# Attention and routing in one pipeline: scatters in later slots, heads through three banks, row maxima turned by VectorE

## The reference

```python
h = h + attn(_layernorm(h))                 # 16 heads of 32, 4 key/value heads, rotary
scores = softmax(q k^T / sqrt(32)); out = scores v; h += out Wo^T
logits = _layernorm(h) @ gate_w.T           # 64 experts
topk_w, topk_i = top_k(softmax(logits), 6)
slot = place of the token in its expert's buffer of 64, in order of tokens
y = experts(...) combined by topk_w + shared expert
```

## Time and profile before

| | |
|---|---|
| median of 3 runs | 1711.42 us (1710.41 to 1715.89) |
| the profiled execution | 1718.32 us, of it a span of 1716.7 us |
| attention phase in the trace | about 160 to 1078 us |
| experts phase | 1078 us to the end |
| one iteration of the full pipeline | about 103 us |

### The profile page before, as it was taken

How to read it: one execution, slowest core, us unless ns; L and a number is a source line. 1 busy time by engine, 2 the same in 40 slices (tenths; PEclk the granted TensorE clock), 3 DMA queues, 4 the chain that set the end, 5 groups by cost and what they waited for, 6 DMA issues and landing times. The chain is left out here.

```text
span 1716.7 us, 23894 instructions
## 1 busy us (share of the span) xinstructions
PE 1377.3 (80%) x9120; PEld 852.8 (50%) x9120; DVE 764.3 (45%) x1633; ACT 405.0 (24%) x676; POOL 423.5 (25%) x455
## 2 busy tenths in 40 slices
PE   3195788888787887878888850399999999999994
PEld 2194352535345353443534340266666666666663
DVE  7982645454655546656454431323233223232221
ACT  2021132324233242332424310211111111111110
POOL 3000110201115042240504367112222222122221
PEclk6597675878778786878868865599999999999997
DMA  3023211313231242304123140798988989898882
GB/s 96 0 65 84 50 39 35 72 35 96 65 77 36 56 109 56 91 19 107 40 56 91 56 179 21 225 312 252 308 274 297 292 261 331 248 321 273 273 247 33
DMA packets 129837, 239.54 MB, mean 140 GB/s; under 512 B 58056, under 2 KB 64088, under 8 KB 129752
## 3 DMA queue, kind: packets, MB, share of 16 engines
q1 hardware_dynamic: 114232, 214.16, 39.9%
q0 software_dynamic: 15520, 24.22, 7.0%
HBM read 175.66 MB, written 38.90 MB: 125 GB/s over the span
## 5 line engine op out<-in xcount | busy, mean ns | idle before, releaser
L965 DVE TENSOR_REDUCE at_maxes<-at_ps 128x1 f32<-128x384 f32 x384 | 196.5, 553 | 131.9 <-PE at_ps L664 124.8
L819 ACT ACTIVATE bulk<-at_ps 128x1152 f32<-128x1152 f32 x128 | 144.6, 1129 | 419.8 <-PE at_ps L634 418.2
L1330 PE MATMUL mo_ps<-mo_x2s,mo_sgu 128*117 128x384 f32 (+1 forms) x1152 | 221.1, 344 | 0.0
L1330 PEld LDWEIGHTS mo_ps<-mo_x2s,mo_sgu 128*117 128x117 f32 (+1 forms) x1152 | 198.8, 181 | 13.3 <-issue 13.1
L1551 POOL DMA_INDIRECT out_rows<-mo_y,mo_scatter_ix x64 | 91.3, 1427 | 406.0 <-DMA out_rows<-mo_y,mo_scatter_ix 185.8
L664 PE MATMUL at_ps<-at_qb 32*128 32x384 bf16 x384 | 113.6, 419 | 69.4 <-DVE at_maxes L965 55.1
L1131 POOL DMA_INDIRECT slot_table<-at_toki,at_si x144 | 141.7, 984 | 58.4 <-issue 47.1
L1094 POOL TENSOR_TENSOR at_oTs<-at_oT,at_oTs 128x384 fp32r<-128x384 f32 x32 | 31.7, 1004 | 402.9 <-ACT at_oTs L836 402.8
L664 PEld LDWEIGHTS at_ps<-at_qb 32*128 32x128 bf16 x384 | 26.8, 95 | 204.6 <-DVE at_maxes L965 152.0
L625 PE MATMUL at_ps<-WxT,at_xT 128*128 128x512 f32 (+1 forms) x576 | 114.6, 352 | 12.7 <-ACT at_v L866 11.0
L650 PE MATMUL at_ps<-bulk,at_v 128*32 128x384 f32 x768 | 113.0, 683 | 3.2 <-DVE at_oT L979 3.2
(11 more groups left out here) (198 smaller groups left out, 1714.5 us busy)
## 6 DMA issues: line engine op xcount, KB each, us to landing
mo_wgu<-in_L_ffn_w_gate SPq DMA_DIRECT2D x32, 704.0 KB, 6.4
mo_wgu<-in_L_ffn_w_up SPq DMA_DIRECT2D x32, 704.0 KB, 7.7
bulk<-in_L_ffn_w_gate SPq DMA_DIRECT2D x32, 704.0 KB, 7.3
bulk<-in_L_ffn_w_up SPq DMA_DIRECT2D x32, 704.0 KB, 8.6
mo_wd<-in_L_ffn_w_down SPq DMA_DIRECT2D x32, 512.0 KB, 7.9
bulk<-in_L_ffn_w_down SPq DMA_DIRECT2D x32, 512.0 KB, 5.3
at_QT<-at_qhi SPq DMA_DIRECT2D x64, 192.0 KB
rows_scores<-at_x SPq DMA_DIRECT2D x8, 864.0 KB, 3.9
```

The costliest lines, as they stand in the source:

```text
L819: A.activation(PT[:, N % RING, :, :], ps[:, 0:NT, 0:SEQ], ACT.Exp, scale=float(HD) ** -0.5)\
L965: V.tensor_reduce(maxes[:, s, h:h + 1], ps[:, 5 + u % 2, 0:SEQ], AX.X, ALU.max, negate=True)\
L1330: m = M.matmul(ps[0:SW[c], 5 + g, 0:SEQ], sgu[:, wa, g, k, SO[c]:SO[c] + SW[c]], x2s[:, xa, k, :], start=(k3 == 0), stop=(k3 == 3 * KC - 1))
```

## The change

Seven edits, all in `attention_phase`.

1. The scatters of sequence e stand in slots 7 to 12 of GpSimd's program in place of 1 to 6.
2. The routing moves a slot forward: `turn_x2` to slots 2 and 3, `logits` to slot 4, its copy and the largest values to slot 5, the one-hot rows and the mask to slot 6, the gate's exponentials to slot 6.
3. The mask is made by three bf16 additions (three ranks plus three, then two more) in place of a reduction and a cast.
4. `turn_heads` goes through banks 5, 6 and 7; group i waits for group i-3. Groups 0, 1 and 2 stand together.
5. On ScalarE `qhi` comes first, and the bf16 copy follows one group behind, made from `qhi`; the raw products wait for all five (`qb_ready`).
6. The maxima are laid out in 32 columns per part of a sequence, and VectorE transposes them itself in blocks of 32 (`max_row`, behind the maxima of slots 11 and 15). `turn_maxes` and ScalarE's copy are gone, and with them the two waits of TensorE on `mrow_ready`. Four DMAs in place of one put the result into `QT`.
7. On VectorE the first two maxima of a slot come at its head, the next two where all stood before, and in slots 11 and 15 `divide` stands behind those four.

```diff
-        TURN_SLOT = {3: (0, 1), 4: (2, 3)}
+        TURN_SLOT = {2: (0, 1), 3: (2, 3)}
-        STACK = 16 * (2 * 6 + 1)
+        STACK = 16 * (2 * 6 + P // HD)
...
             def stack_max(half):
                 heads = slice(half * NH // 2, (half + 1) * NH // 2)
-                sp.dma_start(QT[SPLIT:QR, heads, :].bitcast(F32), mrow[:, half, :].bitcast(F32)).then_inc(stacked[half], 16)
+                for j in range(P // HD):
+                    sp.dma_start(QT[SPLIT:QR, heads, :].rearrange("p h (s j q) -> p h s j q", s=NT, q=HD)[:, :, :, j, :]
+                                 .bitcast(F32), mrow[HD * j:HD * j + NH // 2, half, :, :]).then_inc(stacked[half], 16)
...
                 if u < 2:
-                    pe.wait_ge(qhi_ready, NTILE * (a + 1))
+                    pe.wait_ge(qb_ready, NTILE * (a + 1))
                     pe.wait_ge(qlo_ready, NTILE * (a + 1))
-                if u == HALF_UNITS:
-                    pe.wait_ge(mrow_ready, 2 * a + 1)
...
             def turn_x(a, k):
                 if k == 0:
                     pe.wait_ge(xn_ready, NT * (a + 1))
-                    wait(pe, mrow_ready, 2 * a)
                     wait(pe, max_ready, UNITS * a)
...
-                if i >= 2:
-                    pe.wait_ge(qlo_ready, NTILE * a + i - 1)
+                if i >= 3:
+                    pe.wait_ge(qlo_ready, NTILE * a + i - 2)
                 for s in range(NT):
-                    m = T.transpose(ps[:, 5 + i % 2, s * P:(s + 1) * P], r1[:, s, r, :], ident[:])
+                    m = T.transpose(ps[:, 5 + i % 3, s * P:(s + 1) * P], r1[:, s, r, :], ident[:])
...
+            def bf16_heads(a, i):
+                r = (REP, 0, 1, 2, 3)[i]
+                act.wait_ge(qhi_ready, NTILE * a + i + 1)
+                A.activation(qb[:, r, :], qhi[:, r, :].bitcast(F32), ACT.Copy).then_inc(qb_ready, 1)
...
+            def max_row(a, half):
+
+                dve.wait_ge(max_ready, UNITS * a + HALF_UNITS * (half + 1))
+                if a >= 1:
+                    dve.wait_ge(stacked[half], STACK * a)
+                V.transpose(mrow[:, half].rearrange("p s h -> p (s h)"), maxes[:, half].rearrange("p s h -> p (s h)"))\
+                    .then_inc(mrow_ready, 1)
...
-                    link(V.tensor_reduce(pos[:], hot[:].rearrange("p (s k) e -> p s e k", s=NT), AX.X, ALU.add), route_step)
-                    V.tensor_copy(mask[:], pos[:]).then_inc(mask_ready, 1)
+                    ranks = hot[:].rearrange("p (s k) e -> p s k e", s=NT)
+                    third = TOPK // 2
+                    link(V.tensor_tensor(threes[:], ranks[:, :, 0:third], ranks[:, :, third:TOPK], ALU.add), route_step)
+                    link(V.tensor_tensor(mask[:], threes[:, :, 0], threes[:, :, 1], ALU.add), route_step)
+                    V.tensor_tensor(mask[:], mask[:], threes[:, :, 2], ALU.add).then_inc(mask_ready, 1)
...
+                    for u in units[0:2]:
+                        row_maximum(a, u)
                     if prev and n - 1 in OUT_SLOT:
                         residual(c, OUT_SLOT[n - 1])
-                    if n % REP == REP - 1:
+                    if n % REP == REP - 1 and n < RAW_FROM:
                         divide(NKV * b + n // REP - 1)
...
-                    for u in units[0:3]:
+                    for u in units[2:4]:
                         row_maximum(a, u)
-                    for u in units[3:]:
+                    if n % REP == REP - 1 and n >= RAW_FROM:
+                        divide(NKV * b + n // REP - 1)
+                    for u in units[4:]:
                         row_maximum(a, u)
+                    if nxt and n in (NH * 3 // 4 - 1, NH - 1):
+                        max_row(a, (n - RAW_FROM) // REP)
...
-                    if prev3 and 1 <= n <= 6:
+                    if prev3 and 7 <= n <= 12:
                         pool.wait_ge(slots_ready, e + 1)
-                        for m in range(3 * (n - 1), 3 * n):
+                        for m in range(3 * (n - 7), 3 * (n - 6)):
```

More of the change, by code:

```diff
@@ L665, in raw @@
                          start=True, stop=True).then_inc(raw_scores, 1)
-            def turn_maxes(a, half):
-                pe.wait_ge(max_ready, UNITS * a + HALF_UNITS * (half + 1))
-                for s in range(NT):
-                    m = T.transpose(ps[0:NH // 2, 5, s * P:(s + 1) * P], maxes[:, s, half * NH // 2:(half + 1) * NH // 2],
-                                    ident[:])
-                m.then_inc(max_turned, 1)
             def turn_x(a, k):
@@ L759, in _ @@
                         turn_x2(d, TURN_SLOT[n][0])
-                    if n == 0 and main:
-                        turn_maxes(b, 1)
-                    if n == NH * 3 // 4 and nxt:
-                        values(G, q)
-                        turn_maxes(a, 0)
                     for u in units[0:2]:
@@ L772, in _ @@
                         turn_heads(a, 1)
-                    if not (n == NH * 3 // 4 and nxt):
-                        values(G, q)
+                        turn_heads(a, 2)
+                    values(G, q)
                     for u in units[2:4]:
@@ L783, in _ @@
                         turn_x(a, 3)
-                    if nxt and n == 7:
-                        turn_heads(a, 2)
                     values(G, q + 1)
-                    if prev2 and n == 5:
+                    if prev2 and n == 4:
                         logits(d)
@@ L820, in exponentials @@
                     .then_inc(probs_ready, 1)
-            def max_row(a, half):
-                act.wait_ge(max_turned, 2 * a + half + 1)
-                if a >= 1:
-                    act.wait_ge(stacked[half], STACK * a)
-                A.activation(mrow[:, half, :], ps[0:NH // 2, 5, 0:SEQ], ACT.Copy).then_inc(mrow_ready, 1)
+            def bf16_heads(a, i):
+                r = (REP, 0, 1, 2, 3)[i]
+                act.wait_ge(qhi_ready, NTILE * a + i + 1)
+                A.activation(qb[:, r, :], qhi[:, r, :].bitcast(F32), ACT.Copy).then_inc(qb_ready, 1)
             def x2_copied(d, k):
@@ L845, in _ @@
                         exponentials(b, n)
-                    if main and n == 0:
-                        max_row(b, 1)
-                    if nxt and n == NH * 3 // 4:
-                        max_row(a, 0)
                     if nxt and n == 0:
@@ L853, in _ @@
                             A.activation(xT[:, 0, k, :], ps[:, 5 + k % 2, 0:SEQ], ACT.Copy).then_inc(xhi_ready, 1)
-                    if prev2 and n == 6:
+                    if prev2 and n == 5:
                         act.wait_ge(logits_ready, d + 1)
@@ L876, in _ @@
                                 act.wait_ge(stacked[1], STACK * a)
-                            A.activation(qb[:, (REP, 0, 1, 2, 3)[i], :], ps[:, 5 + i % 2, 0:SEQ], ACT.Copy)
-                            A.activation(qhi[:, (REP, 0, 1, 2, 3)[i], :], ps[:, 5 + i % 2, 0:SEQ], ACT.Copy)\
+                            A.activation(qhi[:, (REP, 0, 1, 2, 3)[i], :], ps[:, 5 + i % 3, 0:SEQ], ACT.Copy)\
                                 .then_inc(qhi_ready, 1)
-                    if prev2 and n == 8:
+                            if i >= 1:
+                                bf16_heads(a, i - 1)
+                        bf16_heads(a, NTILE - 1)
+                    if prev2 and n == 6:
                         act.wait_ge(gmax_ready, d + 1)
@@ L898, in _ @@
             V.memset(base[:], 0.0)
+            V.memset(maxes[:], 0.0)
             V.memset(ones[:], 1.0)
@@ L953, in q_lo @@
                 dve.wait_ge(qhi_ready, NTILE * a + i + 1)
-                V.tensor_tensor(qlo[:, r, :], ps[:, 5 + i % 2, 0:SEQ], qhi[:, r, :].bitcast(F32), ALU.subtract)\
+                V.tensor_tensor(qlo[:, r, :], ps[:, 5 + i % 3, 0:SEQ], qhi[:, r, :].bitcast(F32), ALU.subtract)\
                     .then_inc(qlo_ready, 1)
@@ L959, in row_maximum @@
                 dve.wait_ge(raw_scores, UNITS * a + u + 1)
-                if u == 0:
-                    wait(dve, max_turned, 2 * a - 1)
-                if u == HALF_UNITS:
-                    wait(dve, max_turned, 2 * a)
-                h = REP * g + r
-                V.tensor_reduce(maxes[:, s, h:h + 1], ps[:, 5 + u % 2, 0:SEQ], AX.X, ALU.max, negate=True)\
-                    .then_inc(max_ready, 1)
+                if u % HALF_UNITS == 0:
+                    wait(dve, mrow_ready, 2 * (a - 1) + half + 1)
+                h = REP * (g % 2) + r
+                V.tensor_reduce(maxes[:, half, s, h:h + 1], ps[:, 5 + u % 2, 0:SEQ], AX.X, ALU.max, negate=True)\
+                    .then_inc(max_ready, 1)
+            def max_row(a, half):
[4 more added lines that the diff above has]
+                    .then_inc(mrow_ready, 1)
             def divide(G):
```

13 lines of the change are left out of this document (7 added, 6 removed).

## The result

The changed kernel takes 1629.42 us (median of 4 runs, 1626.21 to 1636.05), the kernel before 1713.66 in the same session: ratio 0.9515, interval 0.9479 to 0.9551. That is faster, by 84 us by the medians. The forecast was 1641 with a range from 1608 to 1688. The profiled execution took 1628.74 us, of it a span of 1626.9, against 1716.7 before.

What follows compares the result with a forecast made beforehand. TensorE was taken to bound the kernel, losing time to pauses, mostly ended by VectorE, and to a low clock. Iterations gain 75 us, the tail loses 5; net 70 from 1718.3 gives 1648, less 6.9 for the median 1641, range 1608 to 1688.

Steps and rivals of the forecast that it cites:

- Scatters and heads, 2.7 us: Iteration 4, after slot 7's scores: head groups start at once, first raw product at 652.6 in place of 655.26.
- the scatters alone cost 2.0: Slot 7's scores to first raw product: iteration 2, without scatters, takes 9.3 us against 11.3, so scatters cost 2.0.
- Mask and clock, 2.2 and 0.9: From slot 8: the 2.2 us pause before the third raw product goes; the clock rises sooner, gaining 0.9 us.
- The additions, 1.2: VectorE's chain ahead of `q_lo`: the mask's three additions take 1.2 us, between bounds of 0.26 and 2.4.
- Slots 11 and 12, 2.4 and 3.2: Iteration 4: slot 11 falls from 7.79 to 5.4 us, slot 12 from 9.37 to 6.2, if the clock stays up.
- rival A: Clock stays at 1.2 GHz through slots 8 to 12; only 38 of 70 us gained, 1673 us; chance 0.22.
- Slots 15 and 0, taken as 0: Turn to next iteration: `turn_x` 1.7 us sooner, against a longer low clock costing 2.0; taken 0, between -3 and +2.
- Contention, -1.0: `over` in slot 9 and three gate products in slot 10 run beside scatters on VectorE: 1.0 us lost per iteration.
- Rival C: Scatters stop VectorE's maxima in slots 7 to 10, 17.5 us in each of iterations 3 to 7: 1728 us; chance 0.05.
- Iterations and tail: Whole attention phase: iterations -1 to 7 gain 75 us together, the tail after them loses 5, net 70.
- Iteration 0's 9.2 for 9: Iteration 0: slots 11 to 15 fall from 29.74 to 22.4 us, 7.3 less, plus 1.7 with the heads: 9.
- Iteration 7: Iteration 7's gain was put at 3 us, without a working.

Runs made afterwards that it cites:

- the run with the routing back: Changed kernel with the routing a slot later again, mask still by additions and scatters still late: 1628.86 us, ratio 0.9529.
- the second run with the scatters back: Changed kernel with the scatters in slots 1 to 6 again, rerun unchanged in the third group: 1615.45 us, ratio 0.9418 (first run 0.9597).
- the two-bank run: Changed kernel with head transposes through banks 5 and 6 and both copies from PSUM: ratio 0.9670, then 0.9617 (1648.02 us) when rerun.
- the division's run: Changed kernel with `divide` ahead of the maxima in slots 11 and 15 again: ratio 0.9659, then 0.9501 (1627.61 us) when rerun.
- the last run: Changed kernel with next sequence's statistics in slot 4, scatters in slots 7 to 12 only before iteration 8, then 1 to 6: 1611.72 us, ratio 0.9418.
- Four kernels of one group: Changed kernel with one part undone each, first group: scatters back 0.9597, maxima turned by TensorE 0.9751, division ahead 0.9659, two banks 0.9670.

## Why the prediction was right, point by point

**What bounds the kernel.** Right. The experts moved as a block; all of the gain came from TensorE's pauses and clock.

**Scatters and heads, 2.7 us.** Measured 3.0, but the step "the scatters alone cost 2.0" saw half of it. Iteration 2 had no scatters and was 2.0 us quicker to its first raw product, and the same 2.0 stand between a cast of 2.18 and one of 0.18, a cast in the chain ahead of `q_lo`. It begins beside a scatter and ends 0.03 to 0.04 us after the delayed `rope_sum` (647.69 and 647.66 in iteration 4; 542.10 and 542.06 in iteration 3). Late scatters free it (0.18 in the run with the routing back), but so does the routing's move with the scatters in their old slots (0.18 in iterations 2 to 6 of the second run with the scatters back). Of the 3.0 us, the two-bank run keeps 0.9 (11.3 to 10.4); the third bank, with its order of copies, gives 2.1. The prediction gave the pause to the scatters; for it either edit suffices.

**Mask and clock, 2.2 and 0.9.** Slots 8 to 10 gained 2.4 of 3.1 in iteration 4. The pause of 2.2 went as said, so the clock's term was near nothing there; in iteration 3 the same slots gained 5.7 (20.9 to 15.2 us).

**The additions, 1.2.** Measured 1.04. The Trainium skill (VectorE: DVE Perf Modes, tier table) gave an estimate of 0.7 by its two elements a cycle; the trace agrees with that rate (576 elements in 0.46 us, 192 in 0.26), and the fixed part is larger than I counted.

**Slots 11 and 12, 2.4 and 3.2.** Measured 3.0 and 1.5 in iteration 4, and 4.66 and 6.05 us long in iteration 3 where 5.4 and 6.2 were forecast. At full clock slot 12's term is right and slot 11's is 0.7 too small; that the clock stays up was right in two iterations of seven. This is rival A in part: in the other five the clock was low in slot 12, which cost 1.3 to 1.9 us in iterations 1, 4, 5 and 6, about a quarter of A's price. And slot 11's term is not a gain of its own, as the division's run showed: it is the other side of slots 12 and 15.

**Slots 15 and 0, taken as 0.** Measured 1.6. The pause of 2.46 ahead of slot 15's raw products fell to 0.65 and 0.73; against it stands the new wait of `turn_x` of 1.93.

**Contention, -1.0.** Under 0.1 us an iteration: `over` has a mean of 279 ns (260 before), a gate product 287 (266). Rival C fell with it. The Trainium skill (SBUF — State Buffer, who interferes with whom), which the prediction cites, says that a reduction never contends on this chip; the maxima agree (552 ns against 553). It also says that a VectorE operation with two SBUF inputs contends with a GpSimd instruction that reads SBUF. By that rule, the one-hot rows of the last run agree, 2.85 us beside an addition of GpSimd and 1.49 without; that their two inputs are the cause was not tried by itself.

**Iterations and tail.** 72.5 us in iterations -1 to 5, where the working gives 62. Iteration 0's 9.2 for 9 is luck: its slots 11 to 15 were to run at full clock and gain 7.3, but stayed at 0.54 and gained 4.1 (29.74 to 25.62); some 2 more came between its first raw product and slot 11, for which the working has nothing. Iteration 7 gave 8.7 where 3 was taken. Its wait for the mask of 2.2 us is gone, and the granted clock is 1.00 in all of it (0.84 before): that term was mis-sized because it was set down as 3 without a reading of iteration 7's own rows. The tail's -5 was exact at -5.4. The profiled spans lie 89.8 us apart where 70 were summed; of the missing 20, 6.1 are in iteration 3 (slots 8 to 10 as above, and slot 12, 10.84 before and 6.05 after), 5.7 in iteration 7 and 2.9 in iteration 6. The medians came only 12 apart from the forecast, since the profiled execution of before lay 7 above its median and that of after 0.7 below; so much of the closeness is luck.

**What the parts are worth together.** Maxima by VectorE 45 us alone, three banks with their order of copies 17, the division nothing, the late scatters -5 to -7 in the tail. The rest, some 27 us, I put down to the freed GpSimd queue, the cast and the mask, which the routing's and the scatters' moves bring in either order; that number is a difference, not a measurement, it takes for granted that the parts add, and the scatters' move alone on the kernel before wasn't tried.

## What to carry to other kernels

Before an edit is costed, follow the wait it cures back through every queue: a GpSimd backlog here was made by a copy on ScalarE that waited for transposes on TensorE, and an edit for another purpose removed it for free. Two cures for one wait each look worthless when left out singly; take out both, or add them singly to the kernel before. Work moved behind a wait is paid for where the moved piece ends, so sum the next slots too, and repeat a surprising loss on another chip before it is explained.

## What the runs showed of the hardware

- Four kernels of one group showed releases that the trace ascribes to no engine, with exponentials 1.3 to 6.7 us behind their scores, 16 to 32 us together in a profile, at places that recur from iteration to iteration; three of them, run again elsewhere, show none and are 9 to 31 us faster by the ratio (0.0053 to 0.0179). The kernel before was 0.5% slower in that group than in the third. The cause is open.
- In the kernel before, a VectorE cast of 24 elements a partition took 2.18 to 2.21 us in iterations 3 to 5, where it began beside a scatter and ended with the GpSimd addition behind it, 0.41 in iteration 6, where it ended with the scatter, and 0.18 in the other four. Not every scatter does it: in the second run with the scatters back, the casts of iterations 3 to 6 began beside one too (595.22, beside a scatter from 594.40 to 595.37) and kept 0.18. One-hot rows of two SBUF inputs took 1.36 us longer beside such an addition. Reductions from PSUM lost nothing beside scatters (552 ns).
- Iterations of equal code had a granted clock of 0.83 to 0.93 in one execution, and the gains of 17.6 us in iteration 3 and 9.5 in iteration 5 go with it (0.93 and 0.83). In iterations 2 and 6 of the changed kernel slots 8 to 11 took 24.7 and 24.8 us with slot 11 at 1.00, yet slot 12 ran at 1.00 in one and 0.77 in the other; what tips it the runs don't tell.
